# Layer 2 of a graph network: one-hots built two chunks ahead, sums taken three chunks behind

## The reference, cut to what matters

```python
k = x @ W_key + b_key
q = x @ W_query + b_query
v = x @ W_value + b_value
gate = sigmoid(k[dst] + q[src])
msg = gate * v[src]
agg = segment_sum(msg, dst, num_segments=6250)
return agg + x @ W_skip + b_skip
```

## Time and profile before

| | us |
|---|---|
| median of 3 runs | 4708.41 (4699.81 to 4726.12) |
| profiled execution | 4697.9 |
| its span | 4696.3 |
| PE busy | 3708.0 (79%) |
| DVE busy | 2881.5 (61%) |
| POOL busy | 2499.5 (53%) |
| ACT busy | 1611.5 (34%) |
| mean granted clock of PE | 0.92 |

### The profile page before, as it was taken

The page is one execution under the profiler, slowest core; times in us unless marked ns, Lnnn a source line. Parts: engine busy times, 40 slices in busy tenths (PEclk is TensorE's granted clock), DMA queues, the critical chain, the costliest instruction groups (busy, mean ns, idle before and its releaser), DMA issues.

```text
span 4696.3 us, 127256 instructions
## 1 busy us (share of the span) xinstructions
PE 3708.0 (79%) x48218; PEld 3256.7 (69%) x48218; DVE 2881.5 (61%) x3816; ACT 1611.5 (34%) x2668; POOL 2499.5 (53%) x2291
## 2 busy tenths in 40 slices
PE   0777699997999996388888888888866777777396
PEld 0656588886999996366666666666646766676396
DVE  6999888885111103377777777777645666666502
ACT  0333399994000002132322232222214444444200
POOL 0288865665655657676666666666402444444200
PEclk9776799998999998699999999999988999999798
DMA  5501288889999994577777777777625767677596
GB/s 170 225 29 29 66 318 319 325 318 287 403 366 417 417 417 158 170 256 248 242 246 242 248 247 236 245 237 243 208 81 175 269 232 255 222 251 240 162 406 253
DMA packets 430076, 1159.85 MB, mean 247 GB/s; under 512 B 111175, under 2 KB 250422, under 8 KB 422712
## 3 DMA queue, kind: packets, MB, share of 16 engines
q1 hardware_dynamic: 331478, 919.45, 55.5%
q0 software_dynamic: 66016, 114.12, 8.4%
q10 hardware_dynamic: 32256, 121.34, 6.5%
HBM read 791.79 MB, written 364.93 MB: 246 GB/s over the span
## 4 chain that ended last, share of the span: by engine, by line
DMA 28%; issue 23%; PE 18%; POOL 13%; DVE 12%; ACT 2%; POOLq 1%; SPq 1%; ACTq 1%; DVEq 0%
DMA feat_slot<-SK,sidx_p 19%; POOL arena L848 7%; POOL feat_slot L924 5%; DVE arena L2422 4%; PE PS L1265 4%; PE PS L1370 4%; DMA arena<-feat_slot 3%; PE PS L1359 3%; PE PS L1364 3%; DMA hots<-arena 2%; DMA sidx_p<-SK 2%; ACT arena L1766 2%; DVE arena L2374 2%; DVE arena L2357 1%; ACTq L1774 1%
## 5 line engine op out<-in xcount | busy, mean ns | idle before, releaser
L924 POOL DMA_INDIRECT feat_slot<-SK,sidx_p x900 | 1100.8, 1223 | 566.7 <-DMA feat_slot<-SK,sidx_p 274.0
L967 POOL DMA_INDIRECT arena<-tab_l_src,SK x864 | 938.7, 1086 | 462.6 <-issue 255.6
L848 POOL TENSOR_TENSOR arena<-arena 128x448 f16<-128x448 f32 x343 | 363.5, 1060 | 668.7 <-ACT arena L1724 668.5
L1265 PE MATMUL PS<-arena 128*128 128x192 bf16 (+1 forms) x7203 | 616.6, 248 | 103.4 <-DVE arena L2176 62.1
L1265 PEld LDWEIGHTS PS<-arena 128*128 128x128 bf16 x7203 | 607.8, 99 | 110.7 <-DVE arena L2176 62.3
L1432 PE MATMUL PS<-arena 128*128 128x128 f16 x4802 | 459.5, 223 | 134.1 <-DVE arena L2357 73.5
L2422 DVE TENSOR_TENSOR arena<-arena 128x896 f32<-128x896 f32 (+1 forms) x319 | 327.9, 1028 | 352.0 <-ACT arena L1766 308.3
L1751 ACT ACTIVATE arena<-PS 128x512 f32<-128x512 f32 (+1 forms) x319 | 175.3, 550 | 1042.4 <-PE PS L1370 1031.2
L1364 PE MATMUL PS<-arena 128*128 (+1 forms) x4178 | 426.2, 225 | 47.5 <-DVE arena L2391 47.5
L1390 PE MATMUL PS<-arena 128*128 128x384 bf16 x2089 | 414.9, 336 | 35.8 <-DVE arena L2429 35.7
L1436 PE MATMUL PS<-arena 128*128 (+1 forms) x4802 | 438.7, 195 | 0.0
(11 more groups left out here) (274 smaller groups left out, 6386.5 us busy)
## 6 DMA issues: line engine op xcount, KB each, us to landing
arena<-slot_rows SPq DMA_DIRECT2D x343, 448.0 KB, 6.1
arena<-cnt_t SPq DMA_DIRECT2D x147, 896.0 KB, 8.3
hots<-arena ACTq DMA_DIRECT2D x175, 672.0 KB
arena<-hots SPq DMA_DIRECT2D x175, 672.0 KB, 4.6
arena<-cnt_t SPq DMA_DIRECT2D x147, 672.0 KB, 9.8
cnt_t<-arena SPq DMA_DIRECT2D x49, 1568.0 KB
cnt_s<-arena SPq DMA_DIRECT2D x49, 1568.0 KB
arena<-cnt_s SPq DMA_DIRECT2D x49, 896.0 KB, 11.8
```

The lines of the kernel that those rows point to most:

```text
L848: pool.tensor_tensor(halves[i][:, n:2 * n], gated[i], halves[i][:, 0:n], ALU.subtract).then_inc(msg_lo, 1)
L924: pool.indirect_dma_start(feat_slot, bass.IndirectOffsetOnAxis(ap=sidx_p[odd][:, n:n + 1].bitcast(u32), axis=0), fwin[h][:, t * D:(t + 1) ...
L967: pool.indirect_dma_start(qgot[n % 3][:, slot_of[t] * P:(slot_of[t] + 1) * P], None, tab_src[4], bass.IndirectOffsetOnAxis(ap=gidx[odd][:, ...
L1265: last = nc.tensor.matmul(PS[:, at:at + w3], ring[u % RING][:, of:of + P], esplit[:, (i * CH + w) * w3:(i * CH + w + 1) * w3], start=u == ...
```

## The change

In the layer 2 pass, and only there:

- PE sums three chunks behind `meet` instead of two (`LAG = 3`).
- DVE makes the one-hots two chunks ahead (`AHEAD = 2`): those of chunks 0 and 1 of a select window in slots 5 and 6 of the kept window before it, and those of chunks 2 to 6 in slots 0 to 4. So that no slot of the last window asks for a window that isn't there, DVE's last six windows are written out (`tail=True`) and its loop has one turn less.
- `halves` has seven places instead of three, one for each chunk, and the arena is laid out anew for it; ACT's sigmoid waits for POOL's remainder of three chunks before (`msg_lo`) and ACT's copy for the sums of seven chunks before (`agg_made`).
- ACT's `first_part` moves from the end of its window to behind slot 1 of the next.
- POOL keeps all remainders, as before.

```diff
-        gated = [carve(122.5 + 3.5 * i, CH * D) for i in range(3)]
-        halves = [carve(124.25 + 3.5 * i, 2 * CH * D, f16) for i in range(3)]
+        gated = [carve(122.5 + 1.75 * i, CH * D) for i in range(3)]
+        halves = [carve(127.75 + 1.75 * c, 2 * CH * D, f16) for c in range(NC)]
...
+            if turns == 3 and tail:
+                for u in range(7):
+                    body(u, u % 3, u // 2, u % 2 == 0, first=u == 0)
+                with eng.Fori(1, (NB - 1) // 6 - 1) as i:
+                    for r in range(1, 7):
+                        body(i * 6 + r, r % 3, i * 3 + r // 2, r % 2 == 0)
+                for u in range(NB - 6, NB):
+                    body(u, u % 3, u // 2, u % 2 == 0, last=u == NB - 1)
+                return
...
-                        if c >= 2:
-                            add_up(w, c - 2, odd)
+                        if c >= LAG:
+                            add_up(w, c - LAG)
                         elif not first:
-                            add_up(w - 1, NC + c - 2, (odd - 1) % turns)
+                            add_up(w - 1, NC + c - LAG)
...
                     if later(w, c, turns):
-                        act.wait_ge(agg_made, w * NC + (PLACES + c + 1 - turns))
+                        act.wait_ge(msg_lo, w * NC + (PLACES + c + 1 - turns))
...
-                    nc.scalar.activation(halves[i][:, 0:CH * w_], gated[i], ACT.Copy).then_inc(msg_hi, 1)
+                    if later(w, 0, 1):
+                        act.wait_ge(agg_made, w * NC + (PLACES + c + 1 - NC))
+                    nc.scalar.activation(halves[c][:, 0:CH * w_], gated[i], ACT.Copy).then_inc(msg_hi, 1)
...
-                    first_part(w)
+                        if c == 1 and not first:
+                            first_part(w - 1)
...
-                        if not kept:
-                            select_rows(w, c, j)
-                            select_sums(w, c, j)
+                        if kept and not last and c >= NC - AHEAD:
+                            select(w + 1, c - (NC - AHEAD), j)
+                        if not kept and c < NC - AHEAD:
+                            select(w, c + AHEAD, j)
```

More of the change, by code:

```diff
@@ L60 @@
 SEQ = 2 * NC - 1
+AHEAD = 2
+LAG = 3
 PLACES = PAIRS_N * SEQ + NC
@@ L484, in chunk_of, with blocks @@
             return slice(o * CH, (o + 1) * CH)
-        def blocks(eng, body, turns=2):
+        def blocks(eng, body, turns=2, tail=False):
+            if turns == 3 and tail:
[7 more added lines that the diff above has]
+                return
             if turns == 3:
@@ L847, in body @@
                         pool.wait_ge(msg_hi, w * NC + (c + 1))
-                        pool.tensor_tensor(halves[i][:, n:2 * n], gated[i], halves[i][:, 0:n], ALU.subtract).then_inc(msg_lo, 1)
+                        pool.tensor_tensor(halves[c][:, n:2 * n], gated[i], halves[c][:, 0:n], ALU.subtract).then_inc(msg_lo, 1)
                 blocks(pool, body, 3)
@@ L1439, in meet, with add_up @@
                     last.then_inc(pre_made, 1)
-                def add_up(w, c, odd):
+                def add_up(w, c):
                     half = int(c >= 4)
@@ L1448, in add_up @@
                     pe.wait_ge(msg_lo, w * NC + (PLACES + c + 1))
-                    parts = halves[(c + odd) % turns].rearrange("p (s j f) -> p s j f", s=2, j=CH)
+                    parts = halves[c].rearrange("p (s j f) -> p s j f", s=2, j=CH)
                     o = PS[:, 3072 + half * 512:3072 + half * 512 + 2 * w_].rearrange("p (s f) -> p s f", s=2)
@@ L1458, in body @@
                         meet(w, c, odd, j, kept)
-                        if c >= 2:
-                            add_up(w, c - 2, odd)
+                        if c >= LAG:
+                            add_up(w, c - LAG)
                         elif not first:
-                            add_up(w - 1, NC + c - 2, (odd - 1) % turns)
+                            add_up(w - 1, NC + c - LAG)
                 blocks(pe, body, turns)
-                for c in range(NC - 2, NC):
-                    add_up(NB - 1, c, 0)
+                for c in range(NC - LAG, NC):
+                    add_up(NB - 1, c)
             def fast_or_general(k):
@@ L1738, in body @@
                             first_half(w - 1, NC - 1, (odd - 1) % turns)
-                    first_part(w)
+                        if c == 1 and not first:
+                            first_part(w - 1)
                 blocks(act, body, turns)
                 first_half(NB - 1, NC - 1, 0)
+                first_part(NB - 1)
             def edge_pairs():
@@ L2330, in second_part, with select, body @@
                     V.tensor_tensor(ystage[:, 0:w_], y0[:, 0:w_], y0[:, w_:2 * w_], ALU.add).then_inc(zb_kept, 1)
-                def body(w, odd, j, kept, first=False):
+                def select(w, c, j):
+                    select_rows(w, c, j)
+                    select_sums(w, c, j)
+                def body(w, odd, j, kept, first=False, last=False):
                     for c in range(NC):
@@ L2337, in body @@
                             gate(*old)
-                        if not kept:
-                            select_rows(w, c, j)
-                            select_sums(w, c, j)
+                        if kept and not last and c >= NC - AHEAD:
+                            select(w + 1, c - (NC - AHEAD), j)
+                        if not kept and c < NC - AHEAD:
+                            select(w, c + AHEAD, j)
                         if c == 4 and not first:
                             second_part(w - 1)
-                blocks(dve, body, turns)
+                blocks(dve, body, turns, tail=True)
                 for c in range(NC - 2, NC):
```

## The result

The changed kernel takes 4675.25 us in the median of 17 runs, against 4699.81 us of the kernel before in 17 runs: a ratio of 0.9944, with a 95% interval of 0.993 to 0.9958. The medians lie 24.6 us apart (the ratio makes it 26): just faster by the prediction's bound of 23.5 us (by the interval it may also be 20 us, which is under it), less than half of the 65 us that the prediction summed up, and 32 us above its 4643, inside its range. The profiled execution took 4684.2 us. The profile of `e2_ahead_only` was taken in an execution of 6246.6 us and is not read; `e12_ahead_again` is the same kernel with another profile.

A forecast was written before the change was run, and what follows sets the result against it. No engine was full: a latency loop bounded kept slots, one-hots directly ahead of `meet` bounded select slots. 24 pairs x (31.9 - 29.5) = 58 plus 7 for loop turns made 65 us off, giving 4643 us, range 4560 to 4705.

The forecast's parts named there:

- bound of 23.5 us: Whole kernel: a difference within 0.5%, 23.5 us or 1.0 us a pair, counts as no change.
- from the landing to the next t0: Layer 2 pair: one-hots, gates and subtraction from the rows' landing until t0 comes again, 10.2 to 11.3 us, 10.5 taken.
- t0: Layer 2 pair: end of the sums of the select window's first chunk, which lets out the first load of stored one-hots.
- clock falls: Rival, layer 2 pass: PE's new wait drops its clock; pair 30.8 to 32.7 us, middle 4700, no change; chance 0.10.
- DVE wait for the rows at K5: Sixth slot of the kept window: DVE waits for late slot rows ahead of queued gates, 4 to 5 us a pair.
- Landing of the rows: Layer 2 pair: first slot rows issued about t0 + 12, landing between t0 + 17.9 and t0 + 20.1, 19.0 taken.
- The pair: Layer 2 pass: a kept plus a select window takes 29.5 us (28.1 to 31.4) instead of 31.9.
- Loop turns: Six loop turns in the layer 2 pass: 1.2 us less each from 5.0, 7 us in all (0 to 16).
- transfer share: Layer 2 pair, a sign: the transfer queue's busy share rises from 0.76 to about 0.82.
- Compute alone: Layer 2 pair: slots without transfer waits bound a pair at 25.0 to 27.0 us against 31.9.
- first rival: Layer 2 pass: the queue's idle 6 us hides the transfers; pair 25.0 to 27.0 us, kernel 4560 us; chance 0.22.

The follow-up runs named there:

- e2_ahead_only: Kernel before with one-hots two chunks ahead, sums still two chunks behind: 1.001 of the kernel before.
- e12_ahead_again: The kernel of e2_ahead_only (one-hots two chunks ahead, sums two behind) run once more for a profile: 1.0009 of the kernel before.
- e4_small_rows: Changed kernel with each load of slot rows bringing only 128 of 1792 columns, so messages are not the reference's: 0.9808 of the kernel before.
- e6: Changed kernel with SP issuing rows 0 and 1 ahead of one-hot loads 5 and 6 of the kept window: 0.9862 of the kernel before.
- e7: Changed kernel with each load of stored one-hots cut in two, the selections going out without waiting for the sums: 0.9787 of the kernel before.
- e5_store_early: Changed kernel with SP storing the kept window's sums behind the third load of one-hots instead of the fifth: 0.9939 of the kernel before.
- e1_lag_only: Changed kernel with one-hots back in their own slot, sums still three chunks behind: 1.0027 of the kernel before.
- e8_split_between: Changed kernel with one-hot loads cut in two, rows 0 and 1 issued earlier and the kept window's store early: 0.972 of the kernel before.
- e10_loads_alone: The loads of e8_split_between with sums two behind and one-hots in their own slot, as before the change: 0.9993 of the kernel before.

## Why the prediction was wrong in its size

- **What failed:** the term "from the landing to the next t0". Its own parts gave 10.2 to 11.3 us and 10.5 was taken; 11.3 was measured, the top of its range. That is 0.8 us in each of 24 pairs, some 20 us and the largest single piece of the shortfall. What stood there was DVE and POOL excluding each other, not PE's clock (next point).
- **The 11.3 us step by step.** In the pair shown DVE starts on the rows at 4056.77 and on gate S0 at 4064.38, 7.61 us later (7.0 to 7.6 forecast: 1.5 and three slots of 5.5 to 6.1), without a wait between. The three slots take 1.66, 2.76 and 1.66 us; the long one holds the one-hot of sums that POOL's subtraction blocks. From gate S0 to the next t0 are 3.72 us (3.2 to 3.7 forecast), since the subtraction in it is blocked too and takes 1.51 instead of 1.03. No run took POOL's work away, so the price of the exclusion is read from these lengths alone. The clock had no part in it. Of the 17 pairs behind the first that have no loop turn, 12 had a mean granted clock of 0.85 or 0.86 in this stretch and 5 had 1.00; the median of the stretch is 11.3 us in both groups. Here is the same stretch in a pair at 1.00 (first row) and in the pair shown (second row; columns as in the earlier trace rows), and some of DVE's lines in the pair at 1.00, which has the same blocked one-hot:

```profile
3959.94:3971.27 11.33, 8.39 (x165) 7.53 (x162) 11.30 (x18) 5.66 (x11) 5.68 (x5) 1.00 0.52 208
4056.77:4068.10 11.33, 9.10 (x161) 8.66 (x159) 11.29 (x18) 5.85 (x11) 5.68 (x5) 0.85 0.51 201
```

```profile
3959.94 0.69 DVE L2320 TENSOR_SCALAR arena<-arena,pnum 128x1792 bf16<-128x1792 bf16 x1 [3.10 <-DMA arena<-slot_rows]
...
3964.51 1.45 DVE L2379 TENSOR_TENSOR arena<-sd,iota 128x896 bf16<-128x896 bf16 x1
...
3967.55 0.61 DVE L2337 TENSOR_TENSOR arena<-arena,PS 128x448 f32<-128x448 f32 x1
```

  In `e4_small_rows` all 17 such pairs were at 1.00, and the stretch again takes 11.3 us in the median. So the rival "clock falls" saw the fall rightly, but not its price: DVE is busy for 11.29 of the 11.33 us, and PE's slower matmuls fit beside it.
- **The mechanism was right.** A new DVE wait for the rows at K5 (3.75 us a pair, 4 to 5 forecast), PE's wait for one-hots gone. Shortening that wait in two ways (`e6`, `e7`) brought 0.8 and 1.6%, both together with an earlier store 2.2%.
- **Landing of the rows:** issue at t0 + 12 forecast, 12.3 measured in the median (12.2 in the pair shown). DVE starts on them 19.1 us behind t0 in the median and 19.4 in the mean; 19.0 was forecast. The issue was worked out; the 7 us from issue to landing were the middle of two estimates that lie 2.2 us apart, so that part of the hit is partly luck. The 0.4 us in the mean are 10 us over 24 pairs.
- **The pair:** 29.5 forecast, 30.7 measured in the median and 30.9 in the mean, so 24 x 1.0 = 24 us of gain in place of 58. The two terms above give 1.2 to 1.3 of the 1.4 us.
- **Loop turns:** forecast to cost 3.8 us instead of 5.0, measured 3.7 instead of 5.4 (pairs with a turn against those without, in the mean). The change took 10.7 us off them where 7 were forecast: right in direction, and a little better than forecast. 24 + 10.7 and 0.6 in the last window are the 35 us of the pass.
- **The starting point:** 4643 is counted from 4708.41, the median of three runs. The 17 runs of the same kernel have 4699.81, from which the same sum would give 4635. Measured against that the miss is 40 us, not 32.
- **A sign that did not come:** the transfer share was to rise to about 0.82. It is 0.75 in the pair shown, and 0.72 from 3700 to 4350 us in both kernels.
- **The store** was not thought of. DVE waits 27.7 us for it, and `e5_store_early` shows no gain from taking it away while the rows are later still. In `e1_lag_only`, without the wait for the rows, the same wait (44.6 us) stands in front of one-hots that PE needs.
- **From the pass to the kernel:** 35 us in the pass, 24.6 us between the medians, 13.7 between the two profiled executions. The last difference has its place: the changed kernel's pass starts 21.6 us later, although the code before it is the same; behind the pass both take the same (304.8 and 304.7 us). In the linear stage ahead of it PE ran at 1.2 GHz in this execution, and mostly not in that of before (the first row is of before, the second of after):

```profile
3520.00:3560.00 40.00, 29.14 (x245) 28.95 (x245) 17.84 (x36) 19.72 (x27) 0.00 (x0) 0.84 0.18 41
```

```profile
3520.00:3560.00 40.00, 40.00 (x190) 40.00 (x189) 6.67 (x18) 11.18 (x15) 0.00 (x0) 0.50 0.00 1
```

  The same stage starts the pass anywhere from 3574.4 to 3611.9 us in the profiles of the experiments, and it varies with one kernel too: the profiled execution of `e8_split_between`, whose pass starts at 3611.9, took 4600.7 us, its other four runs 4568.0 to 4573.3. So it is most likely a matter of the execution and not of the change. Whether the rest of the gap between 35 and 24.6 us is this or something else stays open.
- **Compute alone at 25.0 to 27.0** was right (26.8 in `e8_split_between`), but the first rival's reason, that the queue idles 6 us and so has room, was not: room in the queue does not help while the loads are let out late. `e4_small_rows` has the smallest transfers and still 29.1.

## What to carry to other kernels

When work is moved ahead, its input must be let out earlier by as much, or the wait only moves to an engine that has other things queued behind it: here the consumer moved two slots forward and the release of its load one slot back. Look for loads that wait for more than their own readers (here three one-hots in one transfer, let out by the last of them), and for the order in the queue that issues them; both were free to change. On top of the change they took off four times what the change itself did (102 and 25 us); without it they gave nothing (`e10_loads_alone`). Test the halves of a change and a smaller step of it: neither half gave anything, and one chunk ahead beat two as long as the loads were late. And before a falling clock is blamed, look for the same stretch at full clock: here it took just as long.

## What the runs showed of the hardware

- POOL's subtraction gets in between two one-hots of DVE when its operand comes ready while the first runs, which no row of before had settled. POOL's instruction starts at 4061.26 and runs its 1.05 us, and DVE's one-hot of sums takes 1.45 us instead of 0.61:

```profile
4060.49 0.93 DVE L2320 TENSOR_SCALAR arena<-arena,pnum 128x1792 bf16<-128x1792 bf16 x1
4061.34 1.45 DVE L2379 TENSOR_TENSOR arena<-sd,iota 128x896 bf16<-128x896 bf16 x1
```

```profile
4061.26 1.05 POOL L860 TENSOR_TENSOR arena<-arena 128x448 f16<-128x448 f32 x1 [0.32 <-ACT arena L1738]
```

- In the other phase the two engines settle into a slot of 1.91 us, POOL blocked in each by the one-hots (1.51 us instead of 1.03), which is the lower end, 1.92, of what the prediction worked out:

```profile
4035.35 1.51 POOL L860 TENSOR_TENSOR arena<-arena 128x448 f16<-128x448 f32 x1 [0.40 <-ACT arena L1738]
4037.26 1.51 POOL L860 TENSOR_TENSOR arena<-arena 128x448 f16<-128x448 f32 x1 [0.40 <-ACT arena L1738]
```

  The Trainium skill, page "SBUF — State Buffer", section "Who interferes with whom", has it that where a DVE instruction needs the port pair that DVE shares with GpSimd, whichever of the two issues first holds it for its whole instruction and the other fully blocks. The trace agrees: 1.45 and 1.51 us above, each once as the loser.
- The granted clock was 1.00 in a pair of before whose waits were about a microsecond or less each. In the pair shown of the changed kernel PE stood idle for 1.56 us up to 4052.18, 1.61 up to 4058.97 and 0.58 up to 4060.99, and the clock was 0.50 from 4061.0 to 4063.8; in another pair, with 1.72 us up to 3953.86 and then 0.84, 0.44 and 0.58 up to 3964.16, it stayed at 1.00. What decides between the two no run here shows.
- A lower clock can be free: at 0.85 and at 1.00 the stretch from the landing of the rows to the next t0 took the same 11.33 us, for DVE was the engine that set it.
